# Ten early head pairs for eight, maxima from the third attention block on, and two kinds of bank copies moved from ScalarE to VectorE

## The chip, the cores and the metric

The kernel runs on one core of one Trainium2 chip. The metric is the device time of one execution in microseconds (us), the median of several runs; lower is better. A core has TensorE (PE), VectorE (DVE), ScalarE (ACT), GpSimd (POOL) and SyncE (SP), which here issues all DMAs. Each engine runs its own instruction list in order, and the engines wait for each other at semaphores written out by hand.

## The reference

The input `x` is 4 x 1024 tokens of 128 features. What is computed, cut to what matters:

```python
xn  = layernorm(x)                                   # mean and variance over 128
zn  = layernorm(xn) * ln_w + ln_b
qkv = zn @ W_qkv + b_qkv                             # 16 heads of 8
s   = softmax(q @ k.T / sqrt(8)) @ v                 # per batch and head, 1024 x 1024
s   = xn + concat(s) @ W_proj + b_proj
lg  = xn @ Wr + br                                   # 8 experts, top 2, softmax over these
g   = silu(sum_e w_e * (gelu(xn @ W1_e + b1_e) @ W2_e + b2_e))
out = x + s * g
```

## The kernel before

There are two stages. The **expert stage** goes through 8 groups of 512 tokens. A group has 32 slots (`HT`), one for each of 8 experts x 4 chunks of 128 hidden features; slot numbers run on over the groups (slot 254 is slot 30 of group 7). In a slot TensorE does the three matmuls of a chunk's first product (lines 947 to 949: each factor is kept as a high and a low part) and, three slots later, those of its second product (L968 to L971, or L963 for a chunk kept in full fp32). ScalarE does two GELUs for a chunk (L823, L826), GpSimd and VectorE in turn subtract high from full (L685, L1272), VectorE weights each expert's result (L1289). Beside it the next group is prepared (`pre`: layernorm, router, q, k, v), which has short dependent steps on VectorE.

The **attention stage** goes through 32 pairs of heads (`PAIRS`) x 8 key tiles (`KT`): 256 blocks, block n = (pair p, tile kt). TensorE writes the scores of 128 keys against 2 x 512 queries for both heads (L1034), in two halves of two banks each; ScalarE takes the exponential of each half (L869, 128 x 1024) into a ring of SBUF tiles; two blocks later TensorE multiplies by the values into one bank, `o_bank` (L1055, "P·V" below, 8 weight loads and matmuls). So P·V of block n - 2 stands at the end of block n in TensorE's program, behind both halves of block n's scores. A column of ones beside the values gives the softmax denominators. After a pair's eighth tile `o_bank` is copied to SBUF (`o_copy`, L860, on ScalarE behind the second block of the next pair), and the next pair's first P·V waits for that copy (semaphore `oe`). SyncE then moves the heads and the denominators out (`sp_heads`), VectorE takes reciprocals (`head_rden`, L1358), and these come back broadcast (`sp_rden_out`, `sp_rden_in`); GpSimd normalises the heads of a whole batch with them (L718).

The exponentials need each query's maximum score beforehand. It comes from a **maxima** matmul for each pair, 128 queries, half of the keys and head (32 a pair, 1024 in all): TensorE writes a bank, VectorE reduces it to one column (L1336 in the expert stage, L1318 in attention). After a pair's 32 reduces VectorE takes the minimum of the negated halves (`half_min`, L1327), GpSimd splits it into three bf16 parts (`neg_parts`, L635 to L641), TensorE turns them (`m_t`, L1010), ScalarE copies the turned 48 x 128 out of the bank (`neg_max_t`, L844), and SyncE stores them to DRAM and loads them as extra rows of the scores' operands.

The maxima of the first `EARLY_PAIRS` pairs are done beside the experts, one or two a slot by `EARLY_AT`, in two banks in turn, with all 128 rows of the operands (unused rows zero, L985). Those of the other pairs are spread evenly over attention blocks 0 to 239 (`singles_upto`): in each block up to two behind the first half of the scores, the rest behind the second (L999, 48 rows, the two heads on different row groups). They use a ring of three banks (`ring`), in which a turn takes a place too: a maximum or a turn waits until the item three places earlier has been read. `min_at` and `turn_at` put a pair's half minimum one block, and its turn two blocks, behind the block that completes it. For the early pairs the slots of the minimum (`EARLY_MIN`), of the parts (one later) and of the turn (`EARLY_TURN`) are written out.

In the last 13 blocks, where no maxima are left, the projection and the output of the first groups run beside attention (`ends`).

Of the kernel before, what the change touches and what calls it, by code (L numbers as in the profile page):

```python
# [54 lines left out]
def attention_and_experts(nc, x, ln_w, ln_b, w_qkv, b_qkv, w_proj, b_proj, w1, b1, w2, b2, w_r, b_r, out):  # L55
# [39 lines left out]
    with ExitStack() as ctx:  # L95
# [88 lines left out]
        MAXES = [(p, t, c) for p in range(PAIRS) for t in range(NT) for c in range(2)]  # L184
        EARLY_PAIRS = 8
        EARLY = EARLY_PAIRS * 4 * NT
        BLOCKS = PAIRS * KT
        MAX_BLOCKS = BLOCKS - 2 * KT
        RING = []
# [5 lines left out]
        def singles_upto(n, half):  # L195

            upto = [min(len(SINGLES), -(-((n + a) * len(SINGLES)) // MAX_BLOCKS)) for a in range(2)]
            return (upto[0], min(upto[0] + 2, upto[1]), upto[1])[half]
# [26 lines left out]

        EARLY_AT = [HT + 4 + (27 * m) // 32 for m in range(EARLY)]
        EARLY_DONE = [EARLY_AT[(p + 1) * 4 * NT - 1] for p in range(EARLY_PAIRS)]
        EARLY_TURN = [2 * HT + 2, 2 * HT + 28, 3 * HT + 26, 4 * HT + 26, 5 * HT + 26, 6 * HT + 26, 7 * HT + 5, 8 * HT + 1]
        EARLY_MIN = [d + 2 for d in EARLY_DONE]
# [279 lines left out]
        def _(sp):  # L509
# [31 lines left out]
            for g in range(1, NG):  # L541
                sp_store_w(sp, g)
                sp_store_qk(sp, g)
                if g == 1:
                    sp.wait_ge(S("ones"), 1)
                    sp.wait_ge(S("max_zero"), 6)
                    sp.wait_ge(S("qp_st"), 2 * QP_ST)
                    for p in range(2):
                        sp_max_rows(sp, p)
                if g in (2, 3):  # L550
                    sp_max_rows(sp, g)
                if g + 1 < NG:
                    sp_load_x(sp, g + 1)
                spread_w(g)
                if g > 2:
                    sp_max_rows(sp, g + 1)
                for p in ([], [], [0], [1], [2], [3], [4], [5, 6])[g]:
                    sp_store_max(sp, p)
            for p in range(2):
                sp_score_rows(sp, p)  # L560
                sp_load_max(sp, p)
            sp_store_max(sp, 7)
            sp.wait_ge(S("qp_st"), NG * QP_ST)
# [7 lines left out]
            for n in range(BLOCKS):  # L571
                p, kt = divmod(n, KT)
                if kt == 1 and 1 <= p < PAIRS - 1:
                    sp_score_rows(sp, p + 1)
                if kt == 4 and 1 <= p < PAIRS - 1:
                    sp_load_max(sp, p + 1)
                for q in range(EARLY_PAIRS, PAIRS):
                    if n == done_block(q) and q + 2 < PAIRS:
                        sp_max_rows(sp, q + 2)
                if n in turn_at:  # L580
                    sp_store_max(sp, turn_at[n])
                if p > 0 and kt == 2:
                    sp_heads(sp, p - 1)
                if p > 0 and kt == 6:
                    sp_rden_out(sp, p - 1)
                if p > 0 and kt == 7:
                    sp_rden_in(sp, p - 1)

# [155 lines left out]
        def _(act):  # L744
# [93 lines left out]

            def neg_max_t(p, early=False):
                m_tr = (b5 if early else ring_bank(("mT", p)))[0:NM, 0:P // 2].bitcast(BF16)  # L840
                act.wait_ge(S("mT"), p + 1)
# [4 lines left out]
            def hi(ns):  # L846
# [3 lines left out]
            expert_phase(experts, pre, first={2 * (n - RAW) + 5: hi([n]) for n in range(RAW, 2 * E)},  # L850
                         extra={EARLY_TURN[p] + 1: [lambda p=p: neg_max_t(p, early=True)] for p in range(EARLY_PAIRS)})


            def o_copy(p):

                act.wait_ge(S("PV"), KT * (p + 1))
                if p > 1:
                    act.wait_ge(S(f"o_st{p % 2}"), 64 * (p // 2))
                    act.wait_ge(S(f"den{p % 2}"), 64 * (p // 2))
                act.activation(o_sb[:, p % 2, :], o_bank[:, :], ACT.Copy).then_inc(S("oe"), 1)  # L860

            for n in range(BLOCKS):
                p, kt = divmod(n, KT)
                for a in range(2):
                    s = 2 * n + a
                    if a == 0 and n >= PR:
# [3 lines left out]
                                   ACT.Exp, scale=SCALE).then_inc(S("P"), 1)  # L870
                if n in turn_at:
                    neg_max_t(turn_at[n])
                if kt == 1 and p > 0:
                    o_copy(p - 1)
            o_copy(PAIRS - 1)

# [264 lines left out]
        def _(dve):  # L1141
# [200 lines left out]

            beside = {}
            for m in range(EARLY):
# [4 lines left out]
            expert_phase(experts, pre, first={2 * (n - RAW) + 6: lo([n]) for n in range(RAW, 2 * E)}, extra=beside)  # L1349


            def head_rden(p):
# [51 lines left out]
            dve.wait_ge(S("vd"), NG)  # L1404
            dve.memset(o_bank[:, :], 0.0).then_inc(S("o_zero"), 1)
            for n in range(BLOCKS):
# [5 lines left out]
                for _, u in halves[0]:  # L1412
                    row_max(u)
                if p > 0 and kt == 5:
                    head_rden(p - 1)
                for step in ends.get(at, []):
                    step()
                for _, u in halves[1]:
                    row_max(u)
                for step in ends.get(at + 1, []):  # L1420
                    step()
# [34 lines left out]
```

## Time and profile before

| | us |
|---|---|
| median of 3 runs (1100.84 to 1102.49) | 1101.2 |
| the profiled execution's own time | 1103.0 |
| its span, first to last instruction | 1101.2 |
| TensorE busy | 1029.3 (93%) |
| VectorE busy | 883.7 (80%) |
| ScalarE busy | 866.9 (79%) |
| GpSimd busy | 368.0 (33%) |

The span is divided at about 513 us: the expert stage before, attention after. A busy share is an average over both. Matmuls overlap each other, so a sum of their durations is more than TensorE's busy time, and the distance between the starts of two that follow is the better measure of what one costs.

### The profile page before, as it was taken

The numbers are of one execution on the slowest core, as the hardware profiler recorded it, in microseconds if no ns is written. First come the engines' busy times: TensorE is split into PE (matmuls) and PEld (weight loads), VectorE is DVE, ScalarE is ACT, GpSimd is POOL, SyncE is SP. The second block draws the span as 40 slices with busy tenths as digits, with TensorE's granted clock in tenths as the row PEclk, the third lists the DMA queues.
The fourth block names the chain that finished last, engine by engine and source line by source line (L and its number), as shares of the span: only waits on it lengthen the run. The fifth ranks groups of instructions, "written<-read, shape, count | busy, mean of one in ns | idle before, by whom it ended". The sixth has DMA issues, their size and how long they took to land.

```text
span 1101.2 us, 17451 instructions
## 1 busy us (share of the span) xinstructions
PE 1029.3 (93%) x5865; PEld 444.1 (40%) x5897; DVE 883.7 (80%) x1589; ACT 866.9 (79%) x1190; POOL 368.0 (33%) x555
## 2 busy tenths in 40 slices
PE   4998999999999999999999999999999999999997
PEld 3675666666666666664222222122222121122222
DVE  5647877787878787765999899989998998899943
ACT  6876667676767677666898998989898989798985
POOL 4786656657666667554001000001000001000010
PEclk9999999999999999999999999999999999999998
DMA  6432221414142232324212221212112221122102
GB/s 183 123 99 68 66 83 31 120 30 121 31 107 50 64 80 51 97 51 120 51 44 53 55 53 39 68 40 54 42 52 51 56 53 42 51 53 54 25 24 82
DMA packets 99410, 72.02 MB, mean 65 GB/s; under 512 B 21693, under 2 KB 83834, under 8 KB 99322
## 3 DMA queue, kind: packets, MB, share of 16 engines
q1 hardware_dynamic: 99322, 70.92, 24.5%
q8 instruction: 47, 0.77, 0.3%
q14 instruction: 41, 0.34, 0.1%
HBM read 53.12 MB, written 15.46 MB: 62 GB/s over the span
## 4 chain that ended last, share of the span: by engine, by line
PE 34%; ACT 8%; DVE 7%; issue 2%; SPq 1%; DMA 0%; POOL 0%; ACTq 0%; DVEq 0%; POOLq 0%
PE psum L1055 17%; PE psum L1034 8%; ACT p_ring L869 8%; PE psum L999 7%; DVE neg_max_half L1318 7%; PE psum L1084 1%; ACT o_sb L860 1%; DMA den<-o_sb 0%; SPq L469 0%; PE psum L1098 0%; PE psum L1010 0%; SPq L473 0%; DVE neg_max_rest L1327 0%; DVE y L1379 0%; POOL h_lo L685 0%
## 5 line engine op out<-in xcount | busy, mean ns | idle before, releaser
L869 ACT ACTIVATE p_ring<-psum 128x1024 f32<-128x1024 f32 x512 | 494.8, 1026 | 59.7 <-PE psum L1034 54.3
L1318 DVE TENSOR_REDUCE neg_max_half<-psum 128x1 f32<-128x512 f32 x768 | 481.6, 681 | 44.5 <-PE psum L999 36.7
L1055 PE MATMUL psum<-p_ring,v_sb 128*9 128x512 f32 x2048 | 269.2, 598 | 0.4 <-ACT o_sb L860 0.3
L823 ACT ACTIVATE h_hi<-psum,cols 128x512 fp32r<-128x512 f32 x192 | 132.4, 690 | 132.2 <-PE psum L949 131.2
L999 PE MATMUL psum<-k_max_stack,q_max_stack 48*128 48x512 bf16 x768 | 202.2, 380 | 16.6 <-DVE neg_max_half L1318 16.3
L1336 DVE TENSOR_REDUCE neg_max_half<-psum 128x1 f32<-128x512 f32 x256 | 169.3, 683 | 51.7 <-PE psum L985 45.0
L685 POOL TENSOR_TENSOR h_lo<-h_split,h_hi 128x512 fp32r<-128x512 f32 x128 | 165.1, 1294 | 135.4 <-ACT h_split L826 135.2
L1034 PE MATMUL psum<-q_stack,k_stack 51*128 51x512 bf16 x1024 | 200.0, 386 | 3.4 <-ACT p_ring L869 2.2
L635 POOL CAST neg_max_parts<-neg_max_rest 128x16 bf16<-128x16 f32 x32 | 6.3, 197 | 493.6 <-DVE neg_max_rest L1327 493.5
L1034 PEld LDWEIGHTS psum<-q_stack,k_stack 51*128 51x128 bf16 x1024 | 49.5, 93 | 299.2 <-ACT p_ring L869 276.2
L947 PE MATMUL psum<-xn_t_hi,w_hi 128*128 128x512 f32 x256 | 144.8, 566 | 0.7 <-DVE neg_max_half L1336 0.5
L826 ACT ACTIVATE h_split<-psum,cols 128x512 f32<-128x512 f32 x192 | 131.5, 685 | 0.0
L949 PE MATMUL psum<-xn_t_lo,w_hi 128*128 128x512 f32 x256 | 102.6, 401 | 0.0
L948 PE MATMUL psum<-xn_t_hi,w_lo 128*128 128x512 f32 x256 | 101.8, 398 | 0.0
L1272 DVE TENSOR_TENSOR h_lo<-h_split,h_hi 128x512 fp32r<-128x512 f32 x64 | 56.8, 888 | 51.9 <-ACT h_split L826 51.8
L985 PE MATMUL psum<-k_max_stack,q_max_stack 128*128 128x512 bf16 x224 | 82.9, 387 | 13.1 <-DVE neg_max_half L1336 12.2
L971 PE MATMUL psum<-h_lo,w_hi 128*128 128x512 f32 x192 | 77.5, 403 | 5.1 <-POOL h_lo L685 2.8
L968 PE MATMUL psum<-h_hi,w_hi 128*128 128x512 f32 x192 | 76.8, 400 | 0.0
L969 PE MATMUL psum<-h_hi,w_lo 128*128 128x512 f32 x192 | 76.1, 396 | 0.0
L999 PEld LDWEIGHTS psum<-k_max_stack,q_max_stack 48*128 48x128 bf16 x768 | 52.4, 94 | 55.6 <-DVE neg_max_half L1318 49.2
L676 POOL TENSOR_TENSOR acc<-acc,prod 128x512 f32<-128x512 f32 x48 | 64.9, 1352 | 12.2 <-DVE prod L1289 12.0
L963 PE MATMUL psum<-h_full,w_full 128*128 128x512 f32 x128 | 65.4, 592 | 0.0
(129 smaller groups left out, 957.5 us busy)
## 6 DMA issues: line engine op xcount, KB each, us to landing
expert_w_bc<-expert_w_dram SPq DMA_DIRECT2D x64, 256.0 KB, 5.1
k_rows_dram<-qk_parts SPq DMA_DIRECT2D x24, 256.0 KB, 3.1
q_max_stack<-q_rows_dram SPq DMA_DIRECT2D x64, 96.0 KB, 2.5
k_max_stack<-k_rows_dram SPq DMA_DIRECT2D x64, 96.0 KB, 2.5
q_stack<-q_rows_dram SPq DMA_DIRECT2D x64, 96.0 KB, 2.4
k_stack<-k_rows_dram SPq DMA_DIRECT2D x64, 96.0 KB, 2.5
q_rows_dram<-qk_parts SPq DMA_DIRECT2D x8, 384.0 KB, 2.6
xz<-in_L_attn_z_dram SPq DMA_DIRECT2D x8, 256.0 KB, 3.2
```

The costliest lines, as they stand in the source:

```text
L685: pool.tensor_tensor(hl[:, (g * HS + j) % HR, :], h32[:, (g * HS + j) % FR, :], hh[:, (g * HS + j) % HR, :].bitcast(F32), ALU.subtract)\
L823: act.activation(hh[:, (g * HS + j) % HR, :], up, ACT.Gelu, bias=col(C_B1 + i))\
L826: act.activation(h32[:, (g * HS + j) % FR, :], up, ACT.Gelu, bias=col(C_B1 + i))\
L869: act.activation(p_sb[:, n % PR, a, :, :].rearrange("p h t -> p (h t)"), scores_bank[s % 2], ACT.Exp, scale=SCALE).then_inc(S("P"), 1)
L947: pe.matmul(o, w1h[:, e, ws], G(xh, g), start=True, stop=False)
L948: pe.matmul(o, w1l[:, e, ws], G(xh, g), start=False, stop=False)
L949: pe.matmul(o, w1h[:, e, ws], G(xl, g), start=False, stop=True).then_inc(S("h"), 1)
L999: pe.matmul(ring_bank(("max", u))[:, :], q_m[rows, p % 2, t * P:(t + 1) * P], k_m[rows, p % 2, hh, c * TG:(c + 1) * TG], start=True, stop= ...
L1034: i = pe.matmul(scores_bank[s % 2][:, hh * TG:(hh + 1) * TG], k_s[rows, slot, kt * P:(kt + 1) * P], q_s[rows, slot, a * TG:(a + 1) * TG], ...
L1055: i = pe.matmul(o_bank[at:at + VR, :], v_sb[:, b * KT + kt, 2 * (p % PB) + hh, :], p_sb[:, n % PR, a, hh, :], start=(kt == 0), stop=(kt == ...
L1318: dve.tensor_reduce(mx[:, p % MXR, c, hh * NT + t:hh * NT + t + 1], ring_bank(("max", u)), AX.X, ALU.max, negate=True).then_inc(S("R"), 1)
L1336: dve.tensor_reduce(mx[:, p % MXR, c, hh * NT + t:hh * NT + t + 1], early_bank[m % 2], AX.X, ALU.max, negate=True).then_inc(S("R"), 1)
```

## The change

Ten pairs are early in place of eight: 320 maxima over the same slots, 704 left for attention, which now start at block 2 (`MAX_FROM`) and end at block 239 as before. The slots of the early turns and SyncE's places for the rows of pairs 2 to 11 and for the stores of early maxima follow. In attention both copies out of banks move from ScalarE to VectorE: `o_copy` behind the first reduces of a pair's third block (kt = 2), `neg_max_t` behind the last reduce of its block. Only the last pair's `o_copy` and the early turns' copies stay on ScalarE. The reciprocals move from kt = 5 to 6 and SyncE's steps after them accordingly, and the zeroing of `o_bank` moves into the expert stage.

```diff
-        EARLY_PAIRS = 8
+        EARLY_PAIRS = 10
         BLOCKS = PAIRS * KT
+        MAX_FROM = 2
         MAX_BLOCKS = BLOCKS - 2 * KT
         def singles_upto(n, half):
-            upto = [min(len(SINGLES), -(-((n + a) * len(SINGLES)) // MAX_BLOCKS)) for a in range(2)]
+            upto = [min(len(SINGLES), -(-max(0, n + a - MAX_FROM) * len(SINGLES) // (MAX_BLOCKS - MAX_FROM)))
+                    for a in range(2)]
             return (upto[0], min(upto[0] + 2, upto[1]), upto[1])[half]
-        EARLY_AT = [HT + 4 + (27 * m) // 32 for m in range(EARLY)]
+        EARLY_AT = [HT + 4 + (27 * m) // 40 for m in range(EARLY)]
-        EARLY_TURN = [2 * HT + 2, 2 * HT + 28, 3 * HT + 26, 4 * HT + 26, 5 * HT + 26, 6 * HT + 26, 7 * HT + 5, 8 * HT + 1]
+        EARLY_TURN = [g * HT + at for g, at in ((1, 28), (2, 26), (3, 26), (3, 30), (4, 26), (5, 26), (5, 30), (6, 26),
+                                                (7, 9), (7, 30))]
...
     # SyncE, expert stage, group g
-                if g in (2, 3):
-                    sp_max_rows(sp, g)
+                for p in {2: [2], 4: [5], 6: [8]}.get(g, []):
+                    sp_max_rows(sp, p)
                 if g + 1 < NG:
                     sp_load_x(sp, g + 1)
                 spread_w(g)
-                if g > 2:
-                    sp_max_rows(sp, g + 1)
-                for p in ([], [], [0], [1], [2], [3], [4], [5, 6])[g]:
+                for p in {2: [3], 3: [4], 4: [6], 5: [7], 6: [9]}.get(g, []):
+                    sp_max_rows(sp, p)
+                for p in {2: [0], 3: [1], 4: [2, 3], 5: [4], 6: [5, 6], 7: [7, 8]}.get(g, []):
                     sp_store_max(sp, p)
+            sp_max_rows(sp, EARLY_PAIRS)
...
     # SyncE, attention, block n = (p, kt)
-                if p > 0 and kt == 2:
+                late = p < PAIRS - 1
+                if p > 0 and kt == 2 + late:
                     sp_heads(sp, p - 1)
-                if p > 0 and kt == 6:
+                if p > 0 and kt == 6 + late:
                     sp_rden_out(sp, p - 1)
-                if p > 0 and kt == 7:
-                    sp_rden_in(sp, p - 1)
+                if p > 1 and kt == 0:
+                    sp_rden_in(sp, p - 2)
+            sp_rden_in(sp, PAIRS - 2)
...
     # ScalarE, attention
-                if n in turn_at:
-                    neg_max_t(turn_at[n])
-                if kt == 1 and p > 0:
-                    o_copy(p - 1)
-            o_copy(PAIRS - 1)
+            act.wait_ge(S("PV"), BLOCKS)
+            act.wait_ge(S(f"o_st{(PAIRS - 1) % 2}"), 64 * ((PAIRS - 1) // 2))
+            act.wait_ge(S(f"den{(PAIRS - 1) % 2}"), 64 * ((PAIRS - 1) // 2))
+            act.activation(o_sb[:, (PAIRS - 1) % 2, :], o_bank[:, :], ACT.Copy).then_inc(S("oe"), 1)
...
     # VectorE
+            def o_zero():
+                dve.wait_ge(S("vd"), NG)
+                dve.memset(o_bank[:, :], 0.0).then_inc(S("o_zero"), 1)
+            beside = {(NG - 1) * HT + 2: [o_zero]}
...
+            def neg_max_t(p):
+                m_tr = ring_bank(("mT", p))[0:NM, 0:P // 2].bitcast(BF16)
+                dve.wait_ge(S("mT"), p + 1)
+                dve.wait_ge(S(f"m_st{p % 2}"), 16 * (p // 2))
+                dve.tensor_copy(nmT[:, p % 2, :], m_tr).then_inc(S("mTc"), 1)
+            def o_copy(p):
+                dve.wait_ge(S("PV"), KT * (p + 1))
+                if p > 1:
+                    dve.wait_ge(S(f"o_st{p % 2}"), 64 * (p // 2))
+                    dve.wait_ge(S(f"den{p % 2}"), 64 * (p // 2))
+                dve.tensor_copy(o_sb[:, p % 2, :], o_bank[:, :]).then_inc(S("oe"), 1)
...
             dve.wait_ge(S("vd"), NG)
-            dve.memset(o_bank[:, :], 0.0).then_inc(S("o_zero"), 1)
             for n in range(BLOCKS):
...
                 for _, u in halves[0]:
                     row_max(u)
-                if p > 0 and kt == 5:
+                if p > 0 and kt == 2:
+                    o_copy(p - 1)
+                if p > 0 and kt == (6 if p < PAIRS - 1 else 5):
                     head_rden(p - 1)
                 for step in ends.get(at, []):
                     step()
                 for _, u in halves[1]:
                     row_max(u)
+                if n in turn_at:
+                    neg_max_t(turn_at[n])
```

## Rows read from the trace of the kernel before

**Rows 1.** Page, part 1: busy us (share of the span) and instructions of each engine.

```profile
PE 1029.3 (93%) x5865; PEld 444.1 (40%) x5897; DVE 883.7 (80%) x1589; ACT 866.9 (79%) x1190; POOL 368.0 (33%) x555
```

**Rows 2.** Stretches: length, busy us of each engine, granted clock, DMA share, GB/s.

```profile
524.67:1047.89 523.22, 495.77 (x3597) 106.03 (x3596) 477.95 (x805) 468.83 (x523) 32.71 (x103) 1.00 0.19 49
518.00:524.67 6.67, 6.46 (x35) 1.16 (x34) 5.02 (x9) 4.71 (x6) 0.00 (x0) 0.74 0.86 249
...
77.90:512.73 434.83, 416.11 (x1701) 278.31 (x1734) 327.10 (x618) 293.61 (x510) 274.94 (x363) 0.99 0.27 70
```

**Rows 3.** Groups by line: shapes, count, busy us, mean ns, idle before.

```profile
L869 ACT ACTIVATE p_ring<-psum 128x1024 f32<-128x1024 f32 x512 | 494.8, 1026 | 59.7 <-PE psum L1034 54.3 <-issue 0.5
L1318 DVE TENSOR_REDUCE neg_max_half<-psum 128x1 f32<-128x512 f32 x768 | 481.6, 681 | 44.5 <-PE psum L999 36.7
...
L1336 DVE TENSOR_REDUCE neg_max_half<-psum 128x1 f32<-128x512 f32 x256 | 169.3, 683 | 51.7 <-PE psum L985 45.0 <-remote 6.5
...
L860 ACT ACTIVATE o_sb<-psum 128x512 f32<-128x512 f32 x32 | 19.2, 600 | 4.2 <-PE psum L1055 4.2
...
L844 ACT ACTIVATE neg_max_t<-psum 48x128 bf16<-48x128 bf16 x32 | 8.4, 262 | 2.1 <-PE psum L1010 2.1
...
L1373 DVE COPY msa_t<-psum 16x512 f32<-16x512 f32 x1 | 0.7, 678 | 1.9 <-PE psum L1073 1.9
```

**Rows 4.** Timeline of attention: start us, us, instruction; P·V of consecutive blocks.

```profile
643.92 1.05 PE L1055 MATMUL psum<-p_ring,v_sb 128*9 128x512 f32 x8
...
646.20 1.04 PE L1055 MATMUL psum<-p_ring,v_sb 128*9 128x512 f32 x8
...
648.96 1.04 PE L1055 MATMUL psum<-p_ring,v_sb 128*9 128x512 f32 x8
...
651.56 1.05 PE L1055 MATMUL psum<-p_ring,v_sb 128*9 128x512 f32 x8
...
653.51 1.05 PE L1055 MATMUL psum<-p_ring,v_sb 128*9 128x512 f32 x8
...
655.56 1.05 PE L1055 MATMUL psum<-p_ring,v_sb 128*9 128x512 f32 x8
...
657.51 1.05 PE L1055 MATMUL psum<-p_ring,v_sb 128*9 128x512 f32 x8
...
660.20 1.05 PE L1055 MATMUL psum<-p_ring,v_sb 128*9 128x512 f32 x8
```

**Rows 5.** The same timeline, around a copy of the heads, and one turn.

```profile
643.13 0.38 PE L999 MATMUL psum<-k_max_stack,q_max_stack 48*128 48x512 bf16 x2
643.18 0.60 ACT L860 ACTIVATE o_sb<-psum 128x512 f32<-128x512 f32 x1
...
643.55 3.88 DVE L1318 TENSOR_REDUCE neg_max_half<-psum 128x1 f32<-128x512 f32 x6 [0.16 <-PE psum L999]
...
646.60 2.44 SPq L473 DMA_DIRECT2D den<-o_sb  x4
...
651.42 0.22 PE L1010 MATMUL psum<-ident_b,neg_max_parts 128*48 128x128 bf16 x1 [0.44 <-DVE neg_max_half L1318]
```

**Rows 6.** Waits: us in total, times, longest us.

```profile
PE psum L985 <- DVE neg_max_half L1336: 12.2, 17, 1.9
...
PE psum L1010 <- POOL neg_max_parts L641: 2.0, 2, 1.6
```

**Rows 7.** Timeline of the expert stage: two early maxima in one slot.

```profile
320.86 0.60 PE L985 MATMUL psum<-k_max_stack,q_max_stack 128*128 128x512 bf16 x2
```

**Rows 8.** Timeline of the expert stage's end: the last early pair.

```profile
506.54 0.40 PE L947 MATMUL psum<-xn_t_hi,w_hi 128*128 128x512 f32 x1
...
506.56 0.17 DVE L1327 TENSOR_TENSOR neg_max_rest<-neg_max_half 128x16 f32<-128x16 f32 x1
...
509.55 0.22 POOL L641 TENSOR_TENSOR neg_max_parts<-neg_max_rest,neg_max_parts 128x16 bf16<-128x16 f32 x1 [0.18 <-POOLq L43]
...
511.50 0.24 PE L1010 MATMUL psum<-ident_b,neg_max_parts 128*48 128x128 bf16 x1
```

More of the change, by code:

```diff
@@ L561, in _ @@
                 sp_load_max(sp, p)
-            sp_store_max(sp, 7)
+            sp_store_max(sp, EARLY_PAIRS - 1)
             sp.wait_ge(S("qp_st"), NG * QP_ST)
@@ L837, in experts @@
                 return plan
-            def neg_max_t(p, early=False):
-                m_tr = (b5 if early else ring_bank(("mT", p)))[0:NM, 0:P // 2].bitcast(BF16)
+            def neg_max_t(p):
+                m_tr = b5[0:NM, 0:P // 2].bitcast(BF16)
                 act.wait_ge(S("mT"), p + 1)
@@ L850, in _ @@
             expert_phase(experts, pre, first={2 * (n - RAW) + 5: hi([n]) for n in range(RAW, 2 * E)},
[L851 to L860, printed above, removed]
+                         extra={EARLY_TURN[p] + 1: [lambda p=p: neg_max_t(p)] for p in range(EARLY_PAIRS)})
             for n in range(BLOCKS):
@@ L1341, in lo @@
                 return [lambda n=n: weights_lo(dve, n) for n in ns]
-            beside = {}
+            def o_zero():
+                dve.wait_ge(S("vd"), NG)
+                dve.memset(o_bank[:, :], 0.0).then_inc(S("o_zero"), 1)
+            beside = {(NG - 1) * HT + 2: [o_zero]}
             for m in range(EARLY):
@@ L1349, in _, with neg_max_t @@
             expert_phase(experts, pre, first={2 * (n - RAW) + 6: lo([n]) for n in range(RAW, 2 * E)}, extra=beside)
+            def neg_max_t(p):
+                m_tr = ring_bank(("mT", p))[0:NM, 0:P // 2].bitcast(BF16)
[8 more added lines that the diff above has]
+                dve.tensor_copy(o_sb[:, p % 2, :], o_bank[:, :]).then_inc(S("oe"), 1)
             def head_rden(p):
```

## The prediction

> **What bounds the kernel now.** I read the share of each engine first: TensorE is busy 93% of the span, VectorE 80%, ScalarE 79% [rows 1]. An average over two unlike stages decides nothing, so I cut the span into stretches [rows 2]. In the expert stage (77.90 to 512.73 us) TensorE is busy 416.1 of 434.8 us, VectorE 327.1: TensorE sets the pace, at a granted clock of 0.99, the upper level of 2.4 GHz. In 235 attention blocks (524.67 to 1047.89 us) TensorE is busy 495.8, VectorE 478.0, ScalarE 468.8 of 523.2 us: none is alone the bound, and the order inside a block decides. So I read the starts of consecutive P·V steps [rows 4]. The reader is to see four lengths: 1.95 and 2.05 us in turn for a block with three maxima (mean 2.0), 2.69 for one with four, 2.76 for one with four and the half minimum, 2.60 for one with a turn. From 643.92 to 646.20 it is 2.28: the block behind a ScalarE copy of the heads (0.60 us at 643.18) [rows 4, 5].
>
> Counting checks this. 768 maxima over 240 blocks are 3.2 a block, so 48 blocks have four and 192 three; 23 of the former carry a half minimum and 23 of the latter a turn (the last pair's come after them). 23 x 2.76 + 25 x 2.69 + 23 x 2.60 + 169 x 2.0 = 528.5 us, and 30 copies at about 0.2 add 6: 534.5 us, where 523.2 x 240 / 235 is 534.4 [rows 2, 4].
>
> **The change, part by part.**
>
> *Attention with fewer maxima.* Ten early pairs leave 1024 - 320 = 704 maxima, over blocks 2 to 239: 2.96 a block. No block has four, 10 have two, 21 have a turn (the 22nd comes in the tail, as the 24th does now). Blocks 5 to 239 are then 204 x 2.0 + 21 x 2.60 + 10 x 1.93 (I take ScalarE's two exponentials, 494.8 us / 512 x 2, as their floor [rows 3]) = 481.9 us, where 523.2 are now. That is 41.3 us less, with the ScalarE copies' share gone too. The block of 1.95 stays: between two P·V starts lie P·V itself (1.05 by its row [rows 4]), two pairs of scores and the maxima, and no ScalarE work that the change removes. Of the 41.3 us, 48 x 0.7 = 34 come from the fours, which VectorE sets (4 x 0.64 us of reduces). Bounds: 36 and 45, for three-maxima blocks 0.02 us up or down.
>
> *The copy of the heads on VectorE.* This is the dearest line of the diff. `o_copy(p - 1)` stands in VectorE's program at the pair's third block, behind that block's first two reduces. TensorE's own next P·V (kt = 0 of the new pair) waits for it, and in TensorE's program behind that P·V stand all later scores and maxima; ScalarE's exponentials wait for those scores. Block kt = 2 of [rows 5] shows the times: the two maxima start at 643.13, VectorE's first reduce at 643.55. Six queued reduces take 3.88, the first 0.68 [rows 3], so 0.64 for each behind it: two end at 644.87. The copy takes 0.68 by the one COPY from a bank that the trace has, 16 x 512 [rows 3] (the partitions differ, the 512 elements don't): to 645.55, and a release of about 0.05 follows. P·V, which starts at 643.92 today [rows 4], would start at 645.60: 1.68 late. Today ScalarE copies at 643.18 to 643.78, just in time. TensorE and ScalarE have 0.1 us of slack in a block (the difference of 2.05 and 1.95) and make it up in the next one or two, so some 1.5 us are lost each time. No other work hides it: scores are two banks deep, ScalarE has done its two exponentials and stands. VectorE's third reduce lies in the wait, but VectorE is not what the rest of the pair waits for. The copy falls in blocks 10, 18 ... 234, 29 times: 43.5 us. Some 3 of these also hold a turn, whose 0.6 us then lie beside the wait: -1.5. So +42. Bounds: 1.3 (the copy as quick as ScalarE's 0.60, full overlap, all slack used) to 1.75 a time: 36 to 51. The last two blocks of this kind (242, 250) have no reduces ahead of the copy: 0.
>
> The trace's COPY of 678 ns is one element a cycle with a fixed part. The Trainium skill (VectorE: DVE Perf Modes, "The TRN2 errata") gives 120 + 512 cycles at 0.96 GHz for a VectorE read of a bank, 658 ns as an estimate by that page, which would take 0.6 us off the sum; its "perf-mode tier table" allows a copy from PSUM up to twice the rate, by which 29 copies would be about 8 us cheaper, but the section on PSUM operands holds fp32 to single rate, and the row agrees with that.
>
> *The turned maxima on VectorE.* 22 copies of 0.26 by ScalarE's row [rows 3], behind the block's last reduce. The turn itself waits in TensorE for a ring bank, and that stays (2.60). VectorE is done with three reduces after 3 x 0.64 = 1.9 of 2.6 us, so it is hidden: 0; if it weren't, 22 x 0.26 = 6. ScalarE loses the same copies, where it has slack: 0 to -3. I take 0.
>
> *Denominators two blocks later, reads of them a block later or more.* The heads' DMAs go with the copy; the reciprocal moves from kt = 5 to 6. Their last issue ends at 649.04, 5.3 us behind ScalarE's copy [rows 5]; behind a copy that ends at 645.5 it is 650.8, and with the stall kt = 6 comes at about 653, so they have 2 us to land. 0, at most 29 x 0.2 = 6 in VectorE, hidden. The reads feed the normalising, due tens of blocks later: 0.
>
> *Start of attention.* No maxima in blocks 0 and 1, and the memset moved ahead. Today 7 maxima (2 x 3.2) stand there, 4.5 us of VectorE's time ahead of the first P·V, where the ring can hold three. But TensorE's clock is 0.74 from 518 to 524.67 [rows 2], and with less work at the start I don't expect it back sooner. -1.5; bounds -4 and +1.
>
> *64 maxima more in the expert stage.* 320 over the same 216 slots, 1.48 a slot for 1.19. Two queued early maxima take 0.60 [rows 7], where one has its 0.38 as in attention [rows 5]: some 0.23 for each more on TensorE, the bound there, so 64 x 0.23 = +14.7. To this come waits for VectorE. TensorE waits 12.2 us for the early banks' reduces today [rows 6]. VectorE has 107.7 us idle in the stage [rows 2] and gets 64 x 0.683 = 43.7 more [rows 3], in just the slots of router, rsqrt and gate chains where it is behind already: I take +9. Bounds: 0, and 29, which is every added maximum at VectorE's 0.683.
> The Trainium skill (TensorEngine Tiling (Array Packing), "Theoretical Speedup") has up to twice the rate for a contraction of 64 rows or fewer. In attention the trace shows that: two maxima in 0.38, from two row groups [rows 5]. The early ones use 128 zero-padded rows and get nothing of it, so the move turns half-price work into full-price work; packed they would be 7.4 us cheaper, which this diff doesn't do.
>
> *Turns of the early pairs.* The last pair's half minimum comes at slot 253, its parts on GpSimd at slot 254, and the turn on TensorE at the head of slot 254 as well, where the last one is at 257 now. Today the minimum is at 506.56, the last part at 509.55 + 0.22, the turn at 511.50, and TensorE begins slot 254's expert matmuls at 506.54 [rows 8]: a turn ahead of them would wait some 3.3 us. The tail has 1 us of such waits today which then go: +2.5. Pairs 0, 6 and 8 have one slot between parts and turn; today's two such waits are 2.0 us [rows 6]: +1. Bounds 0 and 6.
>
> SyncE's loads: pair 8's wait for slot 187 now stands ahead of the load of x for group 7, due at 192. Four issues, some 2 us, fit. 0; at most 2.
>
> **Sum**, against the profiled execution (1103.0 us, span 1101.2): -41.3 + 42 - 1.5 + 14.7 + 9 + 3.5 = +27. The median of the runs is 1101.2, 1.8 below the profiled time: 1128.
>
> **Rivals.**
> 1. *The copy is cheap.* For it: ScalarE's copy of 0.60 costs 0.2 us now. If VectorE reached it before TensorE asks, or the waiting P·V had more slack than I read, the price would be 0.3 a pair, 9 us in place of 42: 1128 - 33 = 1095, faster. It decides when the stall is below 0.57 us a copy (27 / 29 = 0.93 off 1.5). Against: VectorE is strictly in order behind two reduces whose maxima TensorE itself issues 0.8 us before the P·V [rows 5].
> 2. *VectorE becomes the bound of the expert stage.* Each early maximum costs 0.683 and more: +29 + 6 in place of 12.5 there, 1150. For: VectorE at 327 + 44 of 450 us with waits for other engines in its order. Against: 80 us of idle left, spread.
> 3. *No new waits in the expert stage, and the rest at its low ends:* 1128 - 9 - 3.5 (turns) - 2.5 (start) - 6 (stall 1.3) = 1107.
> 4. *Gains and losses cancel*, a stall between: 1101.
>
> **How the numbers follow.** Forecast, with its own range 1112 to 1143: 0.68. Rival 1: 0.12. Rival 2: 0.07. Rival 3: 0.10. Rival 4: 0.03. What a measurement can tell here is 0.2%, 2.2 us. Faster by more: 0.12; within: 0.03; slower: 0.85. The range 1104 to 1143 leaves out rivals 1, 2 and 4.
>
> **What would show it.** The lengths between P·V starts: no 2.69 or 2.76 left; one of about 3.5 us at kt = 2 in each pair, with TensorE waiting there for the VectorE copy; ScalarE idle 1.5 us beside it. Blocks 5 to 239 about as long as now (524 us). The expert stage 27 us longer, its waits for L1336 about 21 us, a wait of 3 us at the last turn. I am wrong if P·V of kt = 0 starts within 0.5 us of where it does now, or if the expert stage grows by 15 or less.

## The result, and the profile after

The changed kernel takes 1152.0 us (median of 4 runs, 1150.91 to 1153.76), the kernel before 1101.1: a ratio of 1.0459, interval 1.0446 to 1.0471. It is 51 us slower, where 27 were forecast, and 9 us beyond the range. The profiled execution took 1151.75 us with a span of 1149.9; before, 1103.0 and 1101.2. The sums below go by the spans, 48.7 us apart. The ratios below leave out one execution of the run e1, which took 1425.8 us at a mean granted clock of 0.66.

Part 1 of its page, busy us of each engine, answers to [rows 1]:

```profile
PE 1039.0 (90%) x5864; PEld 445.7 (39%) x5897; DVE 890.3 (77%) x1642; ACT 852.6 (74%) x1137; POOL 369.2 (32%) x555
```

Every engine is busy for a smaller share of the span, and TensorE's busy time grew by 9.7 us only, so most of the added time is idle time. The stretches answer to [rows 2]: the first expert slot of group 1 to the first scores, and blocks 5 to 239 (columns as there; the clock is the third figure from the end).

```profile
77.42:540.87 463.45, 432.99 (x1768) 282.87 (x1799) 352.35 (x686) 295.47 (x512) 277.80 (x371) 1.00 0.27 69
550.78:1096.71 545.93, 491.51 (x3540) 104.03 (x3537) 462.24 (x797) 454.22 (x471) 30.94 (x95) 0.97 0.18 46
```

The expert stretch was 434.8 us and is 463.5: +28.6. The attention stretch was 523.2 and is 545.9: +22.7, although TensorE is busy 4.3 us less there. Its mean granted clock there went from 1.00 to 0.97. What lies between the two went from 11.94 (512.73 to 524.67) to 9.91 us, -2.0. The rest is -0.6 in the preparation and the tail.

The waits name the causes (us in total, times, longest us):

```profile
ACT p_ring L867 <- PE psum L1031: 91.5, 88, 2.7
...
PE psum L1052 <- DVE o_sb L1366: 42.8, 28, 1.6
...
PE psum L982 <- DVE neg_max_half L1333: 19.0, 30, 1.1
...
PE psum L1007 <- POOL neg_max_parts L647: 4.5, 2, 3.1
```

The second row is new: TensorE's P·V waits 42.8 us in 28 places for VectorE's copy, up to 1.6 us each, where it had waited 0.3 us, once, for ScalarE's. The first row is ScalarE's exponentials waiting for scores, 54.3 us before. The third was 12.2, the fourth 2.0 [rows 6]. The two new kinds of copy by line (shapes, count, busy us, mean ns, idle before):

```profile
L1366 DVE COPY o_sb<-psum 128x512 f32<-128x512 f32 x31 | 21.1, 681 | 0.8 <-PE psum L1052 0.8
...
L1358 DVE COPY neg_max_t<-psum 48x128 bf16<-48x128 bf16 x22 | 4.5, 204 | 2.8 <-PE psum L1007 2.8
```

The copy of the heads takes 681 ns, the row of the trace before said 678 [rows 3]; the turned maxima take 204 ns.

One pair's third block and what follows it, from the timeline (start us, us, instruction), to be read beside [rows 4, 5]:

```profile
560.67 1.05 PE L1052 MATMUL psum<-p_ring,v_sb 128*9 128x512 f32 x8
560.90 2.68 DVE L1315 TENSOR_REDUCE neg_max_half<-psum 128x1 f32<-128x512 f32 x4
...
561.87 0.38 PE L996 MATMUL psum<-k_max_stack,q_max_stack 48*128 48x512 bf16 x2
...
563.50 0.68 DVE L1366 COPY o_sb<-psum 128x512 f32<-128x512 f32 x1
...
564.33 1.68 PE L1052 MATMUL psum<-p_ring,v_sb 128*9 128x512 f32 x8 [1.58 <-DVE o_sb L1366]
...
565.93 0.61 PE L1031 MATMUL psum<-q_stack,k_stack 51*128 51x512 bf16 x2
...
566.33 0.64 PE L996 MATMUL psum<-k_max_stack,q_max_stack 48*128 48x512 bf16 x2
...
566.64 1.94 ACT L867 ACTIVATE p_ring<-psum 128x1024 f32<-128x1024 f32 x2 [2.57 <-PE psum L1031]
566.76 0.64 PE L1031 MATMUL psum<-q_stack,k_stack 51*128 51x512 bf16 x2
...
567.75 1.15 PE L1052 MATMUL psum<-p_ring,v_sb 128*9 128x512 f32 x8
...
569.80 1.05 PE L1052 MATMUL psum<-p_ring,v_sb 128*9 128x512 f32 x8
```

VectorE's reduces run to about 563.5, then its copy to 564.18, and P·V starts at 564.33: 3.66 us behind the P·V before it (560.67), where 2.0 is the rule. That much was forecast. What was not is in the durations of the rows after it. This P·V takes 1.68 us instead of 1.05, the scores 0.61 and 0.64 instead of 0.39, the maxima 0.64 instead of 0.38, and the next P·V comes after 3.42 us (567.75) instead of 2.0; only the one after that is in step again (2.05). TensorE is running at half its clock. The next pair, in the same view of TensorE:

```profile
580.41 1.05 PE L1052 MATMUL psum<-p_ring,v_sb 128*9 128x512 f32 x8
...
584.07 1.05 PE L1052 MATMUL psum<-p_ring,v_sb 128*9 128x512 f32 x8 [1.54 <-DVE o_sb L1366]
585.05 0.39 PE L1031 MATMUL psum<-q_stack,k_stack 51*128 51x512 bf16 x2
...
586.02 1.05 PE L1052 MATMUL psum<-p_ring,v_sb 128*9 128x512 f32 x8
...
588.07 1.05 PE L1052 MATMUL psum<-p_ring,v_sb 128*9 128x512 f32 x8
```

The same pause (580.41 to 584.07), but here the clock holds: P·V 1.05, scores 0.39, next P·V after 1.95. All 29 blocks at kt = 2 are alike, 3.65 or 3.66 us from P·V start to P·V start; what differs is what follows. In ten pairs the granted clock falls right behind the pause, and the next three blocks take 7.70 us on average; in the others they take 6.18. The granted clock of three stretches tells the two cases apart:

```profile
564.90:568.00 3.10, 3.10 (x19) 0.56 (x15) 1.00 (x2) 1.36 (x2) 0.00 (x0) 0.50 0.11 21
581.00:587.00 6.00, 4.46 (x40) 0.90 (x32) 4.77 (x9) 4.27 (x5) 0.00 (x0) 1.00 0.11 30
602.40:605.60 3.20, 3.20 (x15) 0.56 (x15) 1.53 (x3) 1.90 (x2) 0.00 (x0) 0.51 0.12 21
```

It is 0.50, the lower level (1.2 GHz), behind the pauses at 564 and 602, and 1.00 (2.4 GHz) through the one at 584. In the record of the granted clock the lower level appears 10 times in blocks 5 to 239, 37.5 us in all; before, once, for 3.4 us. That one fall stands behind the longest wait that TensorE has in this stretch of the kernel before, and the durations show it (times in the trace before):

```profile
937.56 0.39 PE L999 MATMUL psum<-k_max_stack,q_max_stack 48*128 48x512 bf16 x1 [1.07 <-DVE neg_max_half L1318]
938.37 0.46 PE L999 MATMUL psum<-k_max_stack,q_max_stack 48*128 48x512 bf16 x1 [0.42 <-DVE neg_max_half L1318]
938.76 1.89 PE L1055 MATMUL psum<-p_ring,v_sb 128*9 128x512 f32 x8
```

P·V takes 1.89 us there, not 1.05. So the cost that the prediction left out was to be seen once in the trace that it was made from.

Last, the end of the expert stage, which answers to [rows 8]:

```profile
532.00 0.17 DVE L1324 TENSOR_TENSOR neg_max_rest<-neg_max_half 128x16 f32<-128x16 f32 x1
...
534.96 0.22 POOL L647 TENSOR_TENSOR neg_max_parts<-neg_max_rest,neg_max_parts 128x16 bf16<-128x16 f32 x1 [0.18 <-POOLq L43]
...
535.23 0.24 PE L1007 MATMUL psum<-ident_b,neg_max_parts 128*48 128x128 bf16 x1 [3.09 <-POOL neg_max_parts L647]
...
535.40 0.50 PE L944 MATMUL psum<-xn_t_hi,w_hi 128*128 128x512 f32 x1
```

The turn waits 3.09 us for GpSimd's last part, as forecast (3.3).

### The profile page after: what moved, and what is told of

Its sections match the earlier page's. It is cut to its first block, busy times and chain, and to the rows that moved or that the text cites. A ratio compares the mean times of both kernels' runs of the same rounds, so it can differ in the third digit from the quotient of the medians.

```text
span 1149.9 us, 17450 instructions
## 1 busy us (share of the span) xinstructions
PE 1039.0 (90%) x5864; PEld 445.7 (39%) x5897; DVE 890.3 (77%) x1642; ACT 852.6 (74%) x1137; POOL 369.2 (32%) x555
## 4 chain that ended last, share of the span: by engine, by line
PE 41%; DVE 5%; issue 2%; ACT 2%; SPq 2%; DMA 1%; DVEq 0%; POOL 0%; ACTq 0%; POOLq 0%
PE psum L1052 20%; PE psum L1031 11%; PE psum L996 8%; DVE neg_max_half L1315 4%; ACT p_ring L867 2%; DVE o_sb L1366 1%; SPq L472 1%; PE psum L1081 1%; SPq L476 1%; DMA den<-o_sb 1%; PE psum L1095 0%; SPq L448 0%; PE psum L1007 0%; PE psum L960 0%; DVE y L1395 0%
## 5 line engine op out<-in xcount | busy, mean ns | idle before, releaser
L1052 PE MATMUL psum<-p_ring,v_sb 128*9 128x512 f32 x2048 | 276.3, 612 | 44.3 <-DVE o_sb L1366 42.8
L1031 PE MATMUL psum<-q_stack,k_stack 51*128 51x512 bf16 x1024 | 204.0, 395 | 3.5 <-ACT p_ring L867 2.0
L996 PE MATMUL psum<-k_max_stack,q_max_stack 48*128 48x512 bf16 x704 | 182.8, 391 | 1.9 <-DVE neg_max_half L1315 1.8
L982 PE MATMUL psum<-k_max_stack,q_max_stack 128*128 128x512 bf16 x287 | 99.4, 386 | 22.1 <-DVE neg_max_half L1333 19.0
L1269 DVE TENSOR_TENSOR h_lo<-h_split,h_hi 128x512 fp32r<-128x512 f32 x64 | 54.8, 856 | 48.7 <-ACT h_split L832 48.6
L1052 PEld LDWEIGHTS psum<-p_ring,v_sb 128*9 128x9 f32 x2048 | 31.5, 89 | 134.3 <-ACT p_ring L867 67.3
L982 PEld LDWEIGHTS psum<-k_max_stack,q_max_stack 128*128 128x128 bf16 x320 | 27.0, 96 | 101.5 <-DVE neg_max_half L1333 62.3
```

The costliest lines, as they stand in the source:

```text
L982: pe.matmul(early_bank[m % 2][:, :], q_m[:, p % 2, t * P:(t + 1) * P], k_m[:, p % 2, hh, c * TG:(c + 1) * TG], start=True, stop=True).then ...
L996: pe.matmul(ring_bank(("max", u))[:, :], q_m[rows, p % 2, t * P:(t + 1) * P], k_m[rows, p % 2, hh, c * TG:(c + 1) * TG], start=True, stop= ...
L1031: i = pe.matmul(scores_bank[s % 2][:, hh * TG:(hh + 1) * TG], k_s[rows, slot, kt * P:(kt + 1) * P], q_s[rows, slot, a * TG:(a + 1) * TG], ...
L1052: i = pe.matmul(o_bank[at:at + VR, :], v_sb[:, b * KT + kt, 2 * (p % PB) + hh, :], p_sb[:, n % PR, a, hh, :], start=(kt == 0), stop=(kt == ...
```

## The experiments

Each run stands beside runs of the kernel before on the same chip (medians 1101.6 to 1103.1). "Stretch" is blocks 5 to 239, "expert stretch" that from group 1's first slot to the first scores. Lengths of blocks go from one P·V start to the next, and "at kt = 2" is the mean of the 29 such blocks of the stretch. Stretches, block lengths, waits and falls are those of the one profiled execution of each run.

| run | us | ratio, interval | stretch | at lower clock in it |
|---|---|---|---|---|
| before | 1101.1 | | 523.2 | 3.4 us, once |
| changed kernel | 1152.0 | 1.0459 (1.0446 to 1.0471) | 545.9 | 37.5 us, 10 times |
| e1 copy on ScalarE | 1102.8 | 0.9996 (0.9980 to 1.0011) | 492.8 | none |
| e2 copy ahead of the reduces | 1101.4 | 0.9994 (0.9984 to 1.0005) | 491.2 | none |
| e3 copy between them | 1123.3 | 1.0185 (1.0170 to 1.0200) | 514.3 | none |
| e4 last turn later | 1153.2 | 1.0457 (1.0440 to 1.0474) | 547.5 | 37.5 us, 11 times |
| e5 copy alone | 1164.3 | 1.0586 (1.0536 to 1.0636) | 578.4 | 41.0 us, 8 times |
| e6 nine early, ScalarE | 1093.6 | 0.9925 (0.9903 to 0.9947) | 502.4 | none |
| e7 e2, half reduces early | 1088.4 | 0.9875 (0.9844 to 0.9906) | 491.5 | none |
| e8 e2 and e4 | 1095.5 | 0.9943 (0.9920 to 0.9966) | 491.0 | none |
| e9 e6, copy as in e2 | 1097.1 | 0.9951 (0.9934 to 0.9968) | 506.0 | none |
| e10 copy behind all three | 1192.2 | 1.0821 (1.0789 to 1.0853) | 585.1 | 88.7 us, 25 times |

### The copy's engine

```diff
     # VectorE, from the changed kernel
-                if p > 0 and kt == 2:
-                    o_copy(p - 1)
     # ScalarE, behind the exponentials of block n
+                if kt == 1 and p > 0:
+                    act_o_copy(p - 1)
```

> The changed kernel with one part undone: the copies of the heads are back on ScalarE, behind the exponentials of a pair's second block; the turned maxima stay on VectorE. Theory A (the copy behind two reduces makes TensorE wait 1.6 us in each of 29 pairs, and TensorE's clock falls to its lower level behind some of these pauses): the block at kt = 2 goes from 3.62 to about 2.0 us (-47), the blocks of 3.0 to 3.6 us at kt = 3 go (-17), ScalarE's copies cost 0.2 each again (+6): 1152 - 58 = 1094. Theory B (the falls of the clock come from the thinner attention blocks or from something else, not from the pause): they stay, 1111. Theory C (the loss is in the expert stage and attention gains nothing from fewer maxima): above 1135.

Its stretch, columns as above:

```profile
555.54:1048.38 492.84, 477.28 (x3537) 100.11 (x3536) 444.89 (x768) 463.85 (x500) 31.03 (x95) 1.00 0.20 50
```

The stretch lost 53.1 us and the clock stays at 1.00. So the copy's move carries all that attention lost, and theory B (falls without the pause) and C are out. The time is 1102.8, not 1094: I expected -58 in the stretch, and the other parts of this execution were 5 us longer (expert stretch 466.2 against 463.5, the start 11.2 against 9.9). Between the first expert slot of group 1 and the stretch its clock is at the lower level for 10.2 us, in the changed kernel for 3.4, which can be part of it.

### The copy's place

```diff
+                if p > 0 and kt == 2:
+                    o_copy(p - 1)
                 for _, u in halves[0]:
                     row_max(u)
-                if p > 0 and kt == 2:
-                    o_copy(p - 1)
```

> The changed kernel with the copy of the heads still on VectorE in the same block, but ahead of that block's first two reduces instead of behind them. Theory A (the place is the fault, not the engine): the copy starts when the last P·V of the old pair ends, is done 0.3 us before the next P·V is due, and the reduces start 0.2 us later than now; block kt = 2 about 2.05 us, no falls of the clock: about 1089 to 1096. Rival D (VectorE has no room for 0.68 us more in a block, and the delay comes back at the ring of banks): kt = 2 and kt = 3 together 0.5 us longer per pair, 1106 or more.

```profile
554.34:1045.51 491.17, 475.10 (x3540) 103.57 (x3536) 459.40 (x797) 455.00 (x471) 30.97 (x95) 1.00 0.20 50
```

```profile
PE psum L1052 <- DVE o_sb L1366: 3.4, 18, 0.3
```

The same engine, the same copy, two instructions earlier: 491.2 us, as with ScalarE, waits of at most 0.3 us, and the block at kt = 2 has 2.25 us on average instead of 3.65. The fault is the place, not VectorE. Rival D is out. The total is 1101.4, above the 1089 to 1096 of theory A, again by the parts outside the stretch (10.2 us at the lower clock there, as in e1): attention gains 32 us over the kernel before, and the expert stage takes 30 of them (434.8 to 464.8).

The copy between the two reduces:

```diff
-                for _, u in halves[0]:
-                    row_max(u)
-                if p > 0 and kt == 2:
-                    o_copy(p - 1)
+                for i, (_, u) in enumerate(halves[0]):
+                    row_max(u)
+                    if p > 0 and kt == 2 and i == 0:
+                        o_copy(p - 1)
+                if p > 0 and kt == 2 and not halves[0]:
+                    o_copy(p - 1)
```

> The changed kernel with the copy of the heads between the block's two first reduces: half the wait. Theory A: TensorE waits 1.6 - 0.64 = about 1.0 us, block kt = 2 about 3.0 us, so -19 us; if the falls of the clock come from the length of the pause, they get fewer or go: 1116 to 1125. Theory B (the falls don't hang on the pause): as many as now, 1133.

Stretch and wait:

```profile
553.21:1067.48 514.27, 475.15 (x3544) 102.70 (x3536) 462.57 (x796) 454.93 (x471) 30.98 (x95) 1.00 0.19 48
```

```profile
PE psum L1052 <- DVE o_sb L1366: 26.5, 29, 1.0
```

29 waits of up to 1.0 us, kt = 2 at 3.06 us, and not one fall of the clock. 1123.3 lies in theory A's 1116 to 1125. And behind all three reduces:

```diff
-                if p > 0 and kt == 2:
-                    o_copy(p - 1)
...
                 for _, u in halves[1]:
                     row_max(u)
+                if p > 0 and kt == 2:
+                    o_copy(p - 1)
```

> The changed kernel with the copy of the heads behind all three reduces of the block in place of two: the pause of TensorE goes from 1.6 to about 2.2 us. Theory A (the pause is the price, and the clock falls behind long pauses alone): block kt = 2 about 4.2 us, +17 over 29 blocks; falls of the clock in attention at least as many as the 10 of the changed kernel, so 1169 or more. Rival (the falls come by chance and not by the length of the pause): about 1169 with falls as few as in the run with the copy between the reduces (none), then 1155.

The stretch and, inside it, one place behind a pause; then the wait:

```profile
555.19:1140.29 585.10, 513.81 (x3540) 105.56 (x3538) 462.20 (x797) 454.49 (x471) 31.00 (x95) 0.92 0.17 43
569.90:573.10 3.20, 3.20 (x19) 0.56 (x15) 1.11 (x2) 1.47 (x2) 0.00 (x0) 0.50 0.11 21
```

```profile
PE psum L1052 <- DVE o_sb L1366: 61.5, 29, 2.2
```

29 waits of up to 2.2 us, kt = 2 at 4.25 us, 25 falls, 24 of them right behind such a wait. The four places together are a curve: waits of at most 0.3 us (18 of them, e2) or 1.0 us (29, e3) have no fall behind them, waits of 1.6 us have one in about one place of three (10 of 29), waits of 2.2 us in most (24 of 29).

The sizes separate too. A wait is what the block at kt = 2 has above 2.00. Without any wait the stretch is about 484 us (e2: 491.2 less 29 x 0.25; e3: 514.3 less 29 x 1.06). The changed kernel then has 484 + 29 x 1.65 = 531.9, and 14.0 us are left for 37.5 us at the lower clock. In e10 it is 484 + 29 x 2.25 = 549.3, and 35.8 are left for 88.7 us. So a microsecond at the lower level costs 0.37 and 0.40 us. The blocks behind the pauses say the same without this sum: 7.70 us with a fall and 6.18 without, 1.5 us for each of the ten.

A long wait for the copy is not the only thing that a fall follows. The 25th fall of e10 comes right behind a wait of TensorE for a maximum's reduce (1.56 us, near 957), and the one of the kernel before behind waits of 1.07 and 0.42 us shortly after each other. Both times VectorE was held at the reciprocal by late denominators. In e3 one such wait of 1.39 us, near 836, has no fall behind it. Whether the length of one wait decides or the sum of waits near each other, these runs do not separate.

The Trainium skill (TensorE: Matmul & The Clock Gate, "HAM oscillation — how this bites in real kernels") tells of a kernel whose clock falls behind each wait between groups of matmuls. These runs agree in kind: the clock falls behind waits. They differ in measure: the waits are shorter than in its example, and only some of those of 1.6 us have a fall behind them.

### The copy alone, in the kernel before

```diff
     # kernel before: ScalarE
-                if kt == 1 and p > 0:
-                    o_copy(p - 1)
     # VectorE, behind the reduces of halves[0]
+                if p > 0 and kt == 2:
+                    dve_o_copy(p - 1)
```

> The kernel before with one part of the change alone: VectorE copies the heads' outputs, behind the first two reduces of a pair's third block; eight early pairs, maxima from the first block, turned maxima on ScalarE. Theory A: 29 blocks at kt = 2 get 1.6 us longer (+47), ScalarE's copies at 0.25 go (-7), and TensorE's clock falls behind some of the pauses, 5 to 12 times at 1.3 us (+6 to +16): 1147 to 1157. Theory B (the copy is dear only together with the thinner blocks, whose lost work lets the clock fall): no falls, at most 1141.

```profile
524.68:1103.08 578.40, 511.71 (x3600) 109.67 (x3603) 494.86 (x834) 458.32 (x494) 32.71 (x103) 0.96 0.17 44
```

+55.2 in the stretch: kt = 2 is 3.67 us, and the clock is at its lower level for 41.0 us, in 8 places, of which 7 stand right behind the copy's wait and the eighth behind waits of 0.68 and 0.42 us for reduces. Theory B (falls only with thinner blocks) is out. With 1164 it is 7 us above the range I gave. Its runs spread from 1158 to 1172, more than those of any kernel with a short wait, and the slower ones had the lower mean clock: 1158.1, 1161.0, 1167.5 and 1171.6 us at 0.973, 0.969, 0.963 and 0.961.

### The expert stage

The last early turn:

```diff
-                                                (7, 9), (7, 30))]
+                                                (7, 9), (8, 1))]
```

> The changed kernel with one number changed: the turn of the last early pair three slots later (8 * HT + 1 instead of 7 * HT + 30), as the last one stood before. Theory A: TensorE's wait of 3.5 us at slot 254 (that slot is 5.04 us long) goes, about 1 us of waits in the last slots comes back: -2.5, 1149.5. Rival: the wait is only moved to the first scores, which need the copied maxima: no change, 1152.

```profile
80.45:541.72 461.27, 433.24 (x1767) 282.44 (x1798) 352.92 (x686) 296.08 (x512) 278.34 (x370) 1.00 0.25 68
552.21:1099.70 547.49, 492.00 (x3540) 103.99 (x3536) 462.35 (x797) 454.90 (x471) 30.99 (x95) 0.97 0.17 45
```

The expert stretch is 2.2 us shorter (463.5 to 461.3), the attention stretch 1.6 longer with 11 falls, and the time the same (1153.2). By itself this run decides little: the falls of the clock move the total by as much as the turn does. So the same edit on top of the copy at the head of the block:

```diff
     # e2
-                                                (7, 9), (7, 30))]
+                                                (7, 9), (8, 1))]
```

> The changed kernel with the copy of the heads on VectorE ahead of the first reduces and the last early pair's turn three slots later (8 * HT + 1). With no pauses at kt = 2 to let the clock fall, the 3 us that the expert stage saved in the run with the late turn alone should be seen: 1098.5. Rival: they come back at the first scores: 1101.5.

```profile
77.88:538.32 460.44, 433.08 (x1767) 282.69 (x1798) 352.77 (x685) 294.77 (x512) 277.72 (x371) 1.00 0.26 68
548.42:1039.46 491.04, 475.14 (x3539) 103.68 (x3536) 459.45 (x797) 454.36 (x471) 30.92 (x95) 1.00 0.20 51
```

1095.5 against e2's 1101.4; the expert stretch is 460.4 against 464.8, the attention stretch as it was (491.0, 491.2). The 3 us of the turn are there: from slot 252 to the first scores it is 9.0 us against 11.6. That it is nearly 6 in the medians is not the turn alone. Between the first expert slot of group 1 and the attention stretch e2's profiled execution has 10.2 us at the lower clock, this one 3.4; at 0.37 to 0.40 us for each that is an estimated 2.6 us. Why the clock falls there in one execution and not in the other is open.

How much of the stage's growth is VectorE:

```diff
     # e2, and early_max reads half of each bank: half of each early maximum is left out
-                    dve.tensor_reduce(..., early_bank[m % 2], AX.X, ALU.max,
+                    dve.tensor_reduce(..., early_bank[m % 2][:, 0:TG // 2], AX.X, ALU.max,
```

> The changed kernel with the copy of the heads ahead of the first reduces (the second run of the first set), and the 320 early reduces over 256 of 512 columns: it leaves out half of each early maximum. This takes 0.27 us of VectorE from each, and nothing from TensorE. Theory A: of the 29.6 us by which the expert stage grew (slots 32 to 255, 429.7 to 459.3), 14.7 are TensorE's own matmuls and stay, the rest is waits for VectorE and goes, with those that were there before: the stage takes 435 to 445. Rival E (the rest is something else, of GpSimd or of TensorE itself): above 452.

```profile
77.72:531.31 453.59, 428.74 (x1767) 283.04 (x1798) 290.87 (x685) 295.28 (x512) 275.63 (x371) 1.00 0.26 70
```

VectorE is busy 62.9 us less (353.7 to 290.9) and the expert stretch 11.2 us shorter than e2's (464.8 to 453.6); the times are of two executions. By the measure of the expectation, slots 32 to 255, it went from 460.6 to 449.5: outside theory A's 435 to 445 and below rival E's 452. The direction is A's, the size is not. Of the 11.2 us, 6.1 are idle time of TensorE and 5.1 are busy time, which the theory had left alone, and TensorE still waits 16.7 us for early reduces (19.5 in e2). A likely reason, not shown by a run, is VectorE's place in its own order: where it stands at the router's or the GELU's results, a shorter reduce changes nothing. What share each has is open.

### Nine early pairs

```diff
-        EARLY_PAIRS = 10
+        EARLY_PAIRS = 9
-        MAX_FROM = 2
+        MAX_FROM = 0
-        EARLY_AT = [HT + 4 + (27 * m) // 40 for m in range(EARLY)]
+        EARLY_AT = [HT + 4 + (27 * m) // 36 for m in range(EARLY)]
     # EARLY_TURN: (2, 2), (2, 26), (3, 26), (4, 26), (5, 2), (5, 26), (6, 26), (7, 9), (8, 1);
     # SyncE's places for rows and stores accordingly; copy of the heads on ScalarE as in e1
```

> The changed kernel with the copies of the heads back on ScalarE, nine early pairs in place of ten, with slots for their turns accordingly, and maxima from block 0. 736 maxima over 240 blocks: 16 blocks with four in place of 48 before. Theory A (each early pair costs the expert stage some 13 to 15 us; a block with four costs 0.7): against before, +14 in the expert stage and -22 in attention: 1093 to 1096. Rival: the expert stage's waits grow with the first pair as much as with two, +20 or more: 1100 or more.

```profile
77.73:524.39 446.66, 423.64 (x1736) 279.18 (x1767) 339.60 (x653) 294.56 (x511) 275.96 (x366) 1.00 0.26 69
536.48:1038.86 502.38, 484.41 (x3566) 103.43 (x3562) 459.78 (x795) 464.44 (x500) 31.84 (x99) 1.00 0.19 50
```

Against before +11.9 us in the expert stretch and -20.8 in attention: 1093.6 us, in theory A's range, 0.75% (0.53 to 0.97) faster than before. So the first pair pays. Against e6, e8 with its tenth pair has an expert stretch another 13.8 us longer and attention only 11.3 shorter, but its copy is on VectorE; the next run has nine pairs with the copy there.

The same with the copy on VectorE, in e2's place:

```diff
     # e6
-                if kt == 1 and p > 0:
-                    act_o_copy(p - 1)
     # VectorE, ahead of the reduces of halves[0]
+                if p > 0 and kt == 2:
+                    o_copy(p - 1)
```

> Nine early pairs, maxima from block 0, the last turn at 8 * HT + 1, and the copy of the heads on VectorE ahead of the block's first reduces. In the runs so far ten early pairs gave 455.4 us in the expert stage and 491.0 in blocks 5 to 239, nine gave 441.6 and 502.4 with the copy on ScalarE. Theory A (a copy at the head of the block costs about the same on either engine, 0.2 to 0.25 us): 1092 to 1094.5, as with nine and ScalarE. Rival D (where a block has four maxima VectorE has no room for the copy): up to 1 us for each of the few such blocks at kt = 2, and 1096.

```profile
535.60:1041.60 506.00, 483.42 (x3566) 107.12 (x3562) 473.96 (x823) 455.52 (x472) 31.76 (x99) 1.00 0.20 50
```

506.0 against 502.4, 1097.1 against 1093.6 us (the intervals of the ratios overlap, 0.9951 and 0.9925). The total is rival D's, its mechanism is not shown. Only two of the 29 copies fall in a block with four maxima; these blocks take 3.03 and 3.58 us, where e6 has 2.69 and 3.21, 0.7 us of the 3.6 in all. In most other pairs the copy costs the block at kt = 2 about 0.21 us more and the block at kt = 3 about 0.26 less, where ScalarE's had been. The rest is spread over single blocks (3.39 against 2.60 in block 74), and what holds them is open.

With the copy on VectorE both times, the tenth pair (e8 against e9) makes the expert stage 14.3 us longer (446.2 to 460.4) and attention 15.0 shorter: it neither pays nor costs, and the intervals of the totals overlap (0.9951, 0.9943). The fastest kernel of the study that leaves nothing out is e6, and its interval overlaps that of e8, too.

## Why the prediction was wrong

The direction, the place and the mechanism of the wait were right; the size was not, because one consequence of the forecast wait was missing. By the terms of the sum (+26.4 forecast, +48.7 measured in the span):

- **Attention with fewer maxima**, -41.3: measured about -39 (523.2 to 484). Right, inside the bounds of 36 to 45. Of the missing 2 us, the blocks in which VectorE waits for late denominators are part: four at kt = 7 take 2.35 to 3.02 us and hold 2.3 us of such waits, which I had put at 0 (the trace before has 1.5 us of them in three blocks).
- **The copy behind two reduces**, +42: the wait measures 29 x 1.65 = +48. The working had 1.68 a copy, or 48.7. I then took nearly 0.2 off each for slack made up later, and nothing is made up: where the clock holds, the blocks behind the pause are 1.95 and 2.05 us (584.07, 586.02, 588.07).
- **The clock**, not in the prediction: +14. This is the step that failed. "TensorE and ScalarE have 0.1 us of slack in a block" and "some 1.5 us are lost each time" treat the pause as a sum of durations, taken from rows at the upper level, and my bounds ended at 1.75 us a copy. The runs show 1.65 and, in one pair of three, 1.4 to 1.5 more, all in the next blocks: (48 + 14) / 29 = 2.1 us a copy. The clock held in the stretch before except once, behind its longest wait, a place that the prediction does not use.
- **Turned maxima** 0: right. **Start** -1.5: -2.0.
- **64 early maxima and the early turns**, +27.2: +28.6. TensorE's busy time there grew by 16.9 us against 14.7, its idle time by 11.7 against 12.5. The last turn's wait was 3.09 us against 3.3. TensorE's waits for early reduces rose by 6.8 (12.2 to 19.0) where I took 9. Right.

-39 + 48 + 14 + 28.6 - 2.0 - 0.6 = +49.0, to 0.3 us. The 14 is what is left of the stretch after the first two; that it has this size is borne out by e10 (0.40 us for each at the lower level, 0.37 here) and by the blocks behind the pauses.

Of the rivals, the first (the copy is cheap) is what e2 shows for the other side of the reduces, not for the place that was chosen: two instructions make the difference. The second (VectorE bounds the expert stage) didn't occur: +28.6, not the 50 that it stands for; that the measured 1152 lies near its 1150 is chance. Of the third, the stall at 1.3 us, and of the fourth, gains and losses that cancel, nothing was seen. Without the clock the change would have come to about 1138 by this sum, inside the range; the range had no case for it.

## What to carry to other kernels

Where one engine's step gates TensorE, ask not only how long the step takes but what stands ahead of it in its engine's order at that moment; here 1.3 us of reduces that nobody was waiting for cost 48 us and another 14 by the clock, and moving the copy ahead of them gave 54.8 of these back. Price a new pause of TensorE twice, for its length and for what the clock does behind it, and look at matmul durations behind existing pauses of like length before a bound is set. Moving work out of a stage pays while it removes the stage's long blocks: the ninth pair gave 20.8 us for 11.9, the tenth 15.0 for 14.3.

## What the runs showed of the hardware

TensorE's granted clock fell to its lower level behind pauses of 1.6 us in 10 of 29 places (7 and 11 of 29 in e5 and e4, which have the same pause), and behind pauses of 2.2 us in 24 of 29; behind 29 pauses of 1.0 us it never fell. TensorE is busy for 88 to 92% of these stretches. In the kernel before it fell once, behind waits of 1.07 and 0.42 us. A microsecond at the lower level cost 0.37 to 0.40 us.

Which of the equal pauses of 1.6 us are followed by a fall differs (in the changed kernel those near 564, 602, 640 and 677, every other pair, then none until 786), so the pause's length alone does not decide it. It makes the time itself less steady: the copy alone spreads over 13 us in 4 runs.
